# Causal head-dim-8 attention: batch-wise norms and the first batch's rotary q and k, moved into the cross attention's loop

## Reference, cut to what matters

```python
# b5: cross attention, 4 batches, 512 queries, 32 keys
scores = jnp.einsum('bhqd,bhkd->bhqk', q, k) * scale
attn = jax.nn.softmax(scores, axis=-1)
ctx = jnp.einsum('bhqk,bhkd->bhqd', attn, v)
...
x = _layernorm(x + xattn, axis=-1)      # mean and variance, eps 1e-5
...
# b6: first norm, rotary, causal attention
h = _rmsnorm(x, ln1_w)                  # mean of squares only, eps 1e-5
q = _apply_rope(q, cos, sin)
k = _apply_rope(k, cos, sin)
...
scores = jnp.where(causal[None, None], scores, jnp.finfo(scores.dtype).min)
probs = jax.nn.softmax(scores, axis=-1)
x = x + jnp.einsum('bso,ho->bsh', attn, wo)
```

## Time and profile before

| | |
|---|---|
| time, median of 3 runs | 1933.08 us (1931.77 to 1933.29) |
| profiled execution: its own time | 1930.61 us |
| its span in the trace | 1928.7 us |
| TensorE busy | 1676.0 us (87%) |
| VectorE busy | 1323.5 us (69%) |
| ScalarE busy | 946.3 us (49%) |
| GpSimd busy | 314.3 us (16%) |
| mean granted TensorE clock | 0.942 of full speed |

### The profile page before, as it was taken

The page is one execution under the profiler, slowest core; times in us unless marked ns, Lnnn a source line. Parts: engine busy times, 40 slices in busy tenths (PEclk is TensorE's granted clock), DMA queues, the critical chain, the costliest instruction groups (busy, mean ns, idle before and its releaser), DMA issues.

```text
span 1928.7 us, 24866 instructions
## 1 busy us (share of the span) xinstructions
PE 1676.0 (87%) x8020; PEld 742.3 (38%) x8024; DVE 1323.5 (69%) x3117; ACT 946.3 (49%) x2042; POOL 314.3 (16%) x476
## 2 busy tenths in 40 slices
PE   7799999999999989999899676546877699979998
PEld 2254544544544422222344221222433354534443
DVE  7477767767767768885673699998477577733333
ACT  2556556556545526667433656332243266653333
POOL 0000000000001022210376001000012222103443
PEclk8999999999999989999999888777899799989999
DMA  4000000000001121130000000000100532000000
GB/s 189 1 1 1 1 1 1 1 1 1 1 1 42 31 73 51 46 88 2 1 1 0 1 1 1 1 1 1 66 0 9 132 78 73 3 1 1 1 0 22
DMA packets 19808, 44.62 MB, mean 23 GB/s; under 512 B 3872, under 2 KB 13024, under 8 KB 18912
## 3 DMA queue, kind: packets, MB, share of 16 engines
q1 hardware_dynamic: 18768, 41.46, 7.4%
q10 hardware_dynamic: 912, 1.57, 0.3%
HBM read 32.99 MB, written 9.44 MB: 22 GB/s over the span
## 4 chain that ended last, share of the span: by engine, by line
PE 72%; DVE 18%; ACT 4%; issue 4%; DMA 1%; POOL 1%; SPq 0%; ACTq 0%; POOLq 0%; another core or an unknown queue 0%; DVEq 0%
PE ps L569 8%; PE ps L535 7%; PE ps L547 6%; PE ps L988 5%; PE ps L1026 5%; PE ps L949 5%; PE ps L504 3%; PE ps L1433 3%; PE ps L1434 3%; PE ps L1322 3%; PE ps L1441 3%; PE ps L1333 3%; DVE arena L1772 2%; PE ps L524 2%; DVE arena L1759 2%
## 5 line engine op out<-in xcount | busy, mean ns | idle before, releaser
L1135 DVE TENSOR_REDUCE stat<-ps 128x1 f32<-128x512 f32 (+3 forms) x512 | 278.6, 582 | 92.7 <-PE ps L953 48.4
L1079 ACT ACTIVATE arena<-ps 128x512 f32<-128x512 f32 (+3 forms) x512 | 246.3, 515 | 148.5 <-PE ps L1026 81.6
L681 ACT ACTIVATE arena<-ps,stat 128x544 f32<-128x544 f32 x256 | 180.4, 709 | 227.2 <-DVE stat L723 227.2
L723 DVE TENSOR_REDUCE stat<-ps 128x1 f32<-128x544 f32 x256 | 173.6, 720 | 146.8 <-PE ps L535 146.0
L949 PE MATMUL ps<-arena 72*128 72x128 bf16 (+1 forms) x480 | 162.6, 348 | 22.7 <-DMA arena<-b_parts 16.3
L1026 PE MATMUL ps<-arena 75*128 75x512 bf16 (+1 forms) x480 | 161.2, 340 | 9.7 <-ACT arena L1079 7.4
L535 PE MATMUL ps<-arena 64*128 64x272 f32 x1024 | 155.0, 422 | 12.1 <-ACT arena L681 10.4
L569 PE MATMUL ps<-arena 128*64 128x512 f32 (+1 forms) x640 | 160.0, 612 | 6.3 <-DVE arena L743 5.5
L689 ACT COPY arena<-ps 128x512 f32<-128x512 f32 x256 | 136.9, 593 | 14.8 <-PE ps L547 14.8
L547 PEld LDWEIGHTS ps<-wA_sb,arena 128*128 128x128 f32 x1024 | 114.0, 142 | 68.1 <-issue 67.3
L547 PE MATMUL ps<-wA_sb,arena 128*128 128x128 f32 x1024 | 138.5, 279 | 0.0
(11 more groups left out here) (325 smaller groups left out, 2846.7 us busy)
## 6 DMA issues: line engine op xcount, KB each, us to landing
arena<-b_parts SPq DMA_DIRECT2D x168, 96.0 KB
b_parts<-arena SPq DMA_DIRECT2D x64, 128.0 KB, 1.8
reg<-wM_dram SPq DMA_DIRECT2D x1, 3072.0 KB, 10.1
reg<-wB_dram SPq DMA_DIRECT2D x1, 2048.0 KB, 11.5
reg<-wM_dram SPq DMA_DIRECT2D x1, 2048.0 KB, 16.1
reg<-wD_dram SPq DMA_DIRECT2D x1, 1817.0 KB, 10.8
wF_sb<-wF_dram SPq DMA_DIRECT2D x1, 1476.0 KB, 19.9
reg<-b_parts SPq DMA_DIRECT2D x12, 96.0 KB
```

The lines of the kernel that those rows point to most:

```text
L681: e.activation(prob_of(P, r).rearrange("p (a k) -> p a k", a=2), score_banks(r), ACT.Exp, bias=x_neg[:, at_:at_ + 1], accum_out=x_sums[:, ...
L723: e.tensor_reduce(x_neg[:, n % 4:n % 4 + 1], score_banks(r), AX.XY, ALU.max, negate=True).then_inc(sem("max_done"), 1)
L1079: e.activation(p_t[:, m % 8, q0:T], ps[:, S1 + m % S2, q0:T], ACT.Exp).then_inc(exp_done, 1)
L1135: e.tensor_reduce(nm[:, G % 2, u // 4, u % 4:u % 4 + 1], ps[:, step % S1, 0:keys(u)], AX.X, ALU.max, negate=True).then_inc(max_done, 1)
```

## The change

1. The two stages of norms behind b5 are gone. Each batch is normed inside b5's loop, in three uses of PSUM bank 7: centring ("m"), variance ("s") and mean of squares ("t"). On TensorE m, s and t of batch b stand at `n_` = 12, 13 and 15 + 4b; on ScalarE the squares at 13 and 15 + 4b and the roots at 14 and 16 + 4b; on VectorE the centred copy at 12 + 4b and the products at 14 and 16 + 4b. The one buffer `g_cent` and the one buffer `g_dev` serve all batches. All squares are on ScalarE.
2. The loops run on past step 16 for this. The last "t", that of batch 3, is finished inside b6's loop (`pe_last` and `act_last` at step 2, `dve_last` at step 3).
3. q and k of batch 0 are projected by TensorE at `n_` = 17 and 18 into banks 0 and 1, in turn, read by VectorE at the same steps, and split at `n_` = 19, between `total` of batch 2 and the rest of the tail. The packs follow as soon as their parts are in DRAM.
4. All 24 packs of batch 0 are issued by SP, none by ScalarE.
5. `outp` uses bank 6 alone, since bank 7 is the norms'; it waits for the sum of the batch before.
6. The arena's buffers for b6 have fixed places, so that batch 0's packs and parts don't overlap what b5 still uses; `turned` lies over b5's weights. POOL's memsets wait for b5's last sum.
7. The q projection of batch 1 (step 3 of b6) also waits until the last norm has left bank 7.

```diff
--- before.py
+++ after.py
@@ -836,7 +836,7 @@
-        def narrow(nth, src, src_ready, dst, tag, load, wq, wk, wv, wo, bias_v=None, rope=None, early=None, head=0):
+        def narrow(nth, src, src_ready, dst, tag, load, wq, wk, wv, wo, bias_v=None, rope=None, early=None, head=0, border=None):
...
@@ -860,10 +860,10 @@
             else:
-                c = Carve()
-                quarters = [[c(QUARTER) for _ in range(8)] for _ in range(2)]
-                p_t, vv, parts, comb = c(8 * T), c(8 * T), c(3 * T), c(T)
-                turned, m_sb, m_pad, m_rest = c(2 * T), c(T), c(48), c(16)
+                at_ = lambda a, n: arena[:, a:a + n]
+                quarters = [[at_(13632 + QUARTER * n, QUARTER) for n in range(8)], [at_(QUARTER * n, QUARTER) for n in range(8)]]
+                p_t, vv, parts, comb = at_(8192, 8 * T), at_(21824, 8 * T), at_(25920, 3 * T), at_(12288, T)
+                turned, m_sb, m_pad, m_rest = place["wE"][:, :], at_(27456, T), at_(27968, 48), at_(28016, 16)
...
@@ -927,15 +927,20 @@
             def bank_of(b, j):
-                return 4 + j if b == 0 else 3 if b == 1 and early is not None else 7
+                return j % 2 if b == 0 else 3 if b == 1 and early is not None else 7
...
                     e.wait_ge(*src_ready[b])
+                    if border is not None and b == 1 and j == 0:
+                        e.wait_ge(*border["bank7"])
...
                 else:
-                    e.wait_ge(*src_ready[j])
+                    e.wait_ge(*src_ready[0])
+                    e.wait_ge(sem("b5_shift"), B * QB)
+                    if j >= 2:
+                        e.wait_ge(b7_read, at7["qk", b, j - 2])
...
@@ -994,8 +999,6 @@
                     e.matmul(ps[:, 7, :], wt[wo], ot, start=True, stop=True).then_inc(written, 1)
-                for j in range(0 if early is not None else NQ):
-                    qk(e, 0, j)
...
@@ -1009,6 +1012,8 @@
                         e.matmul(ps[:, 7, :], ones, f_dev, start=True, stop=True).then_inc(written, 1)
+                    if border is not None and step == 2:
+                        border["pe_last"](e)
...
@@ -1051,12 +1056,10 @@
             def act(e):
-                if early is None:
-                    e.wait_ge(parts_out, 16 * 8)
-                    for hg in range(4):
-                        pack(e, 0, 1, hg)
...
                     G, u = step // 16, step % 16
+                    if border is not None and step == 2:
+                        border["act_last"](e)
...
@@ -1150,10 +1153,6 @@
                     e.transpose(ot, comb.rearrange("p c r -> p (c r)")).then_inc(ot_done, 1)
-                if early is None:
-                    for j in range(NQ):
-                        qk_read(e, 0, j)
-                    split(e, 0, (0, 1))
...
@@ -1163,6 +1162,8 @@
                         max_step(e, step)
+                    if border is not None and step == 3:
+                        border["dve_last"](e)
...
@@ -1216,7 +1217,7 @@
                 if early is None:
-                    e.wait_ge(*src_ready[B - 1])
+                    e.wait_ge(sem("b5_sum"), B)
...
@@ -1266,7 +1267,7 @@
                             e.wait_ge(score2, 64 * (b - 2) + 16 * (hg + 1))
-                        for w in range(2 if b or early is not None else 1):
+                        for w in range(2):
...
@@ -1282,6 +1283,8 @@
                 early.update(pool_split=split_0, pe_qk=qk, dve_qk=qk_read, dve=max_step, pe=head_step)
+            if border is not None:
+                border.update(pe_qk=qk, dve_qk=qk_read, split=split)
...
@@ -1901,6 +1904,53 @@
             N5 = B * QB
+            border = {}
+            g_cent, g_dev = cent[:, 0, :], cent[:, 1, :]
+            bank7_w, bank7_r = sem("bank7_written"), sem("bank7_read")
+            w_0, r_0 = len(qk_before), len(at7)
+
+            def g_use(kind, b):
+                return 3 * b + ("m", "s", "t").index(kind) + 1
+
+            def g_norms(b):
+                return [(f_normed, B + 2 * b + k) for k in (1, 2)]
+
+            def g_pe(e, kind, b):
+                if kind == "m":
+                    e.wait_ge(sem("b5_sum"), b + 1)
+                else:
+                    e.wait_ge(f_squared, B + 2 * b + (1 if kind == "s" else 2))
+                e.wait_ge(bank7_r, r_0 + g_use(kind, b) - 1)
+                lhs, rhs = (wt["centre"], x_aux[:, b, :]) if kind == "m" else (ones, g_dev)
+                e.matmul(ps[:, 7, :], lhs, rhs, start=True, stop=True).then_inc(bank7_w, 1)
+
+            def g_square(e, kind, b):
+                if kind == "s":
+                    e.wait_ge(bank7_r, r_0 + g_use("m", b))
+                    if b:
+                        e.wait_ge(*g_norms(b - 1)[1])
+                else:
+                    e.wait_ge(*g_norms(b)[0])
+                e.activation(g_dev, g_cent if kind == "s" else x_cur[:, b, :], ACT.Square).then_inc(f_squared, 1)
+
+            def g_root(e, kind, b):
+                e.wait_ge(bank7_w, w_0 + g_use(kind, b))
+                e.activation(g_dev, ps[:, 7, :], ACT.Ln, bias=v("eps5")).then_inc(bank7_r, 1)
+                e.wait_ge(bank7_r, r_0 + g_use(kind, b))
+                e.activation(g_dev, g_dev, ACT.Exp, scale=-0.5).then_inc(f_rooted, 1)
+
+            def g_centred(e, b):
+                e.wait_ge(bank7_w, w_0 + g_use("m", b))
+                e.tensor_copy(g_cent, ps[:, 7, :]).then_inc(bank7_r, 1)
+
+            def g_scale(e, kind, b):
+                e.wait_ge(f_rooted, B + 2 * b + (1 if kind == "s" else 2))
+                if kind == "s":
+                    e.wait_ge(bank7_r, r_0 + g_use("s", b))
+                    e.tensor_tensor(x_cur[:, b, :], g_cent, g_dev, ALU.mult).then_inc(f_normed, 1)
+                else:
+                    e.scalar_tensor_tensor(out=x_aux[:, b, :], in0=x_cur[:, b, :], scalar=v("m_ln1_w"), in1=g_dev,
+                                           op0=ALU.mult, op1=ALU.mult).then_inc(f_normed, 1)
...
@@ -1928,11 +1978,12 @@
                     e.wait_ge(sem("b5_heads"), b + 1)
-                    if b >= 2:
-                        e.wait_ge(sem("b5_sum"), b - 1)
-                    e.matmul(ps[:, 6 + b % 2, :], wt["c_Wo"], oc[:, b % 2, :], start=True,
+                    if b:
+                        e.wait_ge(sem("b5_sum"), b)
+                    e.matmul(ps[:, 6, :], wt["c_Wo"], oc[:, b % 2, :], start=True,
                              stop=True).then_inc(sem("b5_out"), 1)
-                for n_ in range(N5 + 7):
+                e.wait_ge(sem("load_wF"), 16)
+                for n_ in range(N5 + 10):
...
@@ -1948,20 +1999,29 @@
                         i.then_inc(sem("b5_turn"), 1)
-                    if n_ >= 8 and (n_ - 8) % 4 == 0:
+                    if (n_ - 8) % 4 == 0 and 0 <= (n_ - 8) // 4 < B:
                         pv((n_ - 8) // 4)
-                    if n_ >= 10 and (n_ - 10) % 4 == 0:
+                    if (n_ - 10) % 4 == 0 and 0 <= (n_ - 10) // 4 < B:
                         outp((n_ - 10) // 4)
+                    if n_ in (N5 + 1, N5 + 2):
+                        for j in range(2):
+                            border["pe_qk"](e, 0, 2 * (n_ - N5 - 1) + j)
+                    for kind, at_ in (("m", 12), ("s", 13), ("t", 15)):
+                        if (n_ - at_) % 4 == 0 and 0 <= (n_ - at_) // 4 < B:
+                            g_pe(e, kind, (n_ - at_) // 4)
...
                     e.activation(qc[:, b, :], ps[:, b, :], ACT.Identity, bias=v("c_bq")).then_inc(sem("b5_exp"), 1)
-                for n_ in range(N5 + 3):
+                for n_ in range(N5 + 12):
+                    for step, kind, at_ in ((g_root, "t", 16), (g_square, "s", 13), (g_root, "s", 14), (g_square, "t", 15)):
+                        if (n_ - at_) % 4 == 0 and 0 <= (n_ - at_) // 4 < B:
+                            step(e, kind, (n_ - at_) // 4)
...
                         e.activation(pc[:, n_ % 4, :, :], pc[:, n_ % 4, :, :], ACT.Exp).then_inc(sem("b5_exp"), 1)
-                    if n_ >= 3:
+                    if 3 <= n_ < N5 + 3:
...
@@ -1993,10 +2053,10 @@
                     e.wait_ge(sem("b5_out"), b + 1)
-                    e.scalar_tensor_tensor(out=x_aux[:, b, :], in0=ps[:, 6 + b % 2, :], scalar=v("c_bo"),
+                    e.scalar_tensor_tensor(out=x_aux[:, b, :], in0=ps[:, 6, :], scalar=v("c_bo"),
...
                 hs = lambda x: x.unsqueeze(2).to_broadcast([128, H, S])
-                for n_ in range(N5 + 8):
+                for n_ in range(N5 + 11):
...
@@ -2011,10 +2071,21 @@
                         e.reciprocal(st5[:, 2, a, :], st5[:, 1, a, :]).then_inc(sem("b5_recip"), 1)
-                    if n_ >= 9 and (n_ - 9) % 4 == 0:
+                    if (n_ - 9) % 4 == 0 and 0 <= (n_ - 9) // 4 < B:
                         heads((n_ - 9) // 4)
-                    if n_ >= 11 and (n_ - 11) % 4 == 0:
+                    if (n_ - 11) % 4 == 0 and 0 <= (n_ - 11) // 4 < B:
                         total((n_ - 11) // 4)
```

(25 more changed lines are left out.)

## The result

The kernel with the change takes 1925.80 us, the median of 7 runs (1925.04 to 1927.54); the kernel before, run beside it, 1932.36 us (7 runs, 1931.18 to 1938.44). The ratio is 0.9967, with a 95% interval of 0.9952 to 0.9982: 0.33% faster, 6.6 us.

A forecast was written before the change was run, and what follows sets the result against it. The prediction took the border from b5's last sum to b6's first score, 33.0 us, as serial. Order -10.9 and clock +4.1 gave -6.8 us, so 1926.3 us from a median of 1933.08, range 1917.5 to 1931.

The forecast's parts named there:

- The walk through the border: From b5's step 12 to b6's start: new in-order queues timed on the old trace's clock, batch 1's q matmul at 1496.07.
- The order's term: At batch 1's q matmul in b6: the new order gains 10.9 us if TensorE keeps full clock.
- the late edge: In the norm tail: TensorE's clock falls to 1.2 GHz between 1480 and 1487, the later limit being 1487.
- the term 4.1: In the norm tail: slower norm matmuls at low clock cost 4.1 us, bounds 0 and 4.6, leaving a gain of 6.8.
- The packs were hidden: Before b6's first score: group 0's packs land at about 1490, covered by the norm tail, which holds TensorE until 1491.
- the lower bound of 7.4: Batch 0's packs: group 0 is there at least 7.4 us after the first issue, at most 1.25 us more.
- the same steps at the same 0.50, and the end moves with them: From batch 1's q matmul on: steps and clock as before, so the whole 6.8 us gain reaches the end.
- Rival C: Low clock outlasts b6's step 16 into dense steps: 7 us of it take the gain, 14 give 1940; chance 0.06.
- A: Clock stays up through border and b6's start: gain 13.8 to 16.1 us, 1917 to 1919.3; chance 0.24 with partial form.
- B: In b6, a 5.11 us DMA of row maxima at 1534.52 waits longer and eats the gain: 1930 to 1934; chance 0.06.
- D: In the norm tail: a missed wait holds it 3 to 5 us more, 1929 to 1931; chance 0.09.

The follow-up runs named there:

- experiment 1: Changed kernel plus unread 512-column matmuls into idle bank 3 in the norm tail, run twice: 1922.19 and 1922.16 us (0.9942 and 0.9944 of the kernel before).
- Experiment 5: Unread filler matmuls in the border and behind b6's first 32 scores: changed kernel 1917.38 us (0.9922), kernel before 1927.80 us (0.9967).
- experiment 3: Changed kernel with batch 0's q and k projection, read and split moved behind batch 3's first norm: 1944.52 us, 1.0066 of the kernel before.
- experiment 6: The kernel before, unchanged, run again for a second profile: 1931.25 us, 0.9996 of the kernel before.
- experiment 2: Kernel before plus 18 unread 512-column matmuls while TensorE waits for the packs: 1930.39 us, 0.9998 of the kernel before.
- c4_filled_b6: Changed kernel plus one unread 128-column matmul behind each of b6's first 32 scores, none in the norm tail: 1919.16 us, 0.9931 of the kernel before.
- c2_split_pool: Changed kernel with batch 0's split on GpSimd instead of VectorE, no fillers: 1922.27 us, 0.9948 of the kernel before.

## Why the prediction came out right

1. **The walk through the border held.** Less the offset of 0.42, batch 1's sum came at 1463.11 (walked 1463.19), batch 1's copy at 1467.60 (1467.64), batch 2's sum at 1474.97 (1474.99), the packs at 1481.62 (1481.9). The order's term, 10.9 us at batch 1's q matmul, is met by experiment 1, where nothing is slowed: its q matmul starts at 1494.54, 45.53 after the origin, against 56.52 before, 11.0 less. Experiment 5 shows it end to end, 10.4 us.

2. **The clock fell where it was said, at the late edge (1487.2 on the walk's clock), and its term was too large at that point.** Both matmuls of batch 2's norms still ran at full clock (1.14 each at 1481.85 and 1485.81). The prediction had 0.95 for the one and 0.45 for the other; without them 4.1 becomes 2.7, and 2.7 it was: 48.24 from the origin to the q matmul, against 45.53 in experiment 1. So the gain there was 8.3 and not 6.8 us.

3. **The packs were hidden**, as costed. Group 0 stood under the tail, the first score waited for no DMA, and in experiment 3, where that cover is gone, the first score waits for its packs (6.0 us from the first issue, under the lower bound of 7.4).

4. **The step that was weak: from the q matmul on, the same steps at the same 0.50, and the end moves with them.** It holds for like against like (7.1 us left at batch 2 in experiment 6). It does not hold between the two first traces, where the clock rose at 1521.4 in the one and at 1535.4 in the other: 8.06 at batch 1's mark, 1.45 at batch 2's. The walk took one execution's rise for the kernel's, and put the clock's cost behind the q matmul at nothing. Rival C named this mechanism and put the border at a rise later than 1521.5; the rise was later by 14.0 us, but the like happens to the kernel before as well, so that the comparison keeps most of the gain. That the forecast of 1926.3 lies so near the median is therefore in part luck. With fillers the change wins 8.9 us and the kernel before 4.75, so end to end the clock takes 4.2 of the gain, which has the size of the term 4.1, but is made up otherwise: 2.7 up to the q matmul, the rest behind it. And the baseline moves with the clock: the two traces of the kernel before took 1930.61 us with the early rise and 1938.38 with the late one, and its median lies between them. The Trainium skill (TensorE: Matmul & The Clock Gate, Part 1) has activity release the throttle; the fall in the tail agrees with it, but 11.50 us of full work (1523.70 to 1535.20) passed before the rise, so the measurement shows that this alone doesn't tell when the clock comes back.

5. **The other part between the traces lies in unchanged code.** Of the 3.1 us between the spans, -0.42 is the origin's, 1.45 was left at batch 2's mark (1.46 at batch 3's), and 2.0 come after batch 3's mark. There, too, the clock differs; windows of the kernel before, and under them of the kernel after:

```profile
1700.00:1752.00 52.00, 40.77 (x131) 17.51 (x132) 25.02 (x75) 20.70 (x38) 8.21 (x8) 0.84 0.00 0
```

```profile
1700.00:1752.00 52.00, 39.16 (x129) 16.75 (x129) 25.88 (x76) 20.63 (x37) 9.98 (x9) 0.90 0.00 1
```

6. **Rivals.** A (the clock stays up) did not come about by itself, but its price was right in size: experiment 5 reaches it with fillers, 1917.4 against the 1917 to 1919.3 given. B rested on a misread row. The 5.11 at 1534.52 is a piece of the chain released by a DMA, but no time in which TensorE stood still; the window over it, in the kernel before:

```profile
1534.52:1539.65 5.13, 5.10 (x58) 2.56 (x50) 3.69 (x8) 2.95 (x9) 0.10 (x1) 1.00 0.80 183
```

TensorE is busy 5.10 of 5.13 us, and after the change the piece is absent. There was no stall that could grow; a transfer landing later than it did (at 1539.63, and TensorE took it up at 1539.67) would have made one. D (a missed wait) found nothing: no table load, no DMA, no late memset in the tail.

Open is why the clock comes back 27 us after its fall in one execution of a kernel and 48 us after it in another, and how often each happens; only one profiled execution of each run was seen.

## What to carry to other kernels

Take long transfers out of a serial border by putting them under compute that must run anyway; experiment 3 shows that the compute moved without the transfer only costs. When a border is thinned like this, read the granted clock for all of what follows, and from more than one execution: here, in the changed kernel, the low clock costs nearly as much (8.9 us) as the reordering gains (10.4), in the kernel before about half of that (4.75). Cheap matmuls into an idle bank give it back, in the thin steps behind the border above all; in the wait ahead of them alone they gave nothing (experiment 2). A piece of the chain that is put down to a DMA is a stall only where the window over it shows the engine idle.

## What the hardware showed that was not expected

- Full work did not bring the clock back at once: it stayed at 0.50 for 11.50 us with TensorE busy 11.50 by its records (1523.70 to 1535.20, after), mostly in short bf16 matmuls that contract 72 or 75 rows.
- The same kernel had its clock low for 27 us in one execution and for 48 in another (before: 1494.1 to 1521.4 and 1494.6 to 1542.4), with the same work in the same order. In two variants of the change it was back after 7 us, with fillers (`c4_filled_b6`) and without (`c2_split_pool`); with one 128-column filler behind each score it stayed up, without them it fell twice more.
- With one queue issuing the packs, the first group was there 6.0 us after the first issue (experiment 3); with two queues it had been 7.4, although one queue takes twice as long to issue the six packs of that group. What makes it quicker was not tested.
